# First attention stage: two projection products moved from the head of a turn to places between the score pairs

## The reference, cut to what matters

```python
latent_kv = x @ w_kv_down
k, v = split(latent_kv @ w_kv_up)
q = x @ w_q
att = softmax(where(causal, q @ k.T * 64 ** -0.5, -inf))
y = (att @ v) @ w_out
# beside it, with weights and activations quantised to FP4 in blocks of 16
gate, up = fp4_linear(x, w_gate), fp4_linear(x, w_up)
ffn = fp4_linear(silu(gate) * up, w_down)
x = x + y + ffn
```

## Time and profile before

| | us |
|---|---|
| median of 3 runs | 2572.29 (2571.3 to 2573.58) |
| the profiled execution | 2572.54 |
| its span, first to last instruction | 2570.7 |

### The profile page before, as it was taken

The page is one execution under the profiler, slowest core; times in us unless marked ns, Lnnn a source line. Parts: engine busy times, 40 slices in busy tenths (PEclk is TensorE's granted clock), DMA queues, the critical chain, the costliest instruction groups (busy, mean ns, idle before and its releaser), DMA issues. The chain is left out here.

```text
span 2570.7 us, 49578 instructions
## 1 busy us (share of the span) xinstructions
PE 2252.3 (88%) x19387; PEld 1397.6 (54%) x19387; DVE 1705.0 (66%) x2090; ACT 1371.9 (53%) x2165; POOL 112.4 (4%) x259
## 2 busy tenths in 40 slices
PE   3799999898999999898989955959999999999998
PEld 2466666666666666666666642624444444444444
DVE  8566666666666576666666685067776777777781
ACT  3455555545455554545455541406666566566666
POOL 0100000000000000000000021000000000000000
PEclk8799999999999999999999977959999999999999
DMA  2000000000000000000000007023111111111000
GB/s 75 1 0 0 0 0 0 0 0 0 0 0 0 0 0 0 0 0 0 0 0 0 0 17 175 23 56 59 18 18 25 31 23 18 27 18 32 12 2 10
DMA packets 41101, 41.18 MB, mean 16 GB/s; under 512 B 21393, under 2 KB 33633, under 8 KB 40865
## 3 DMA queue, kind: packets, MB, share of 16 engines
q1 hardware_dynamic: 38904, 36.87, 6.7%
q0 software_dynamic: 640, 1.15, 0.4%
q10 hardware_dynamic: 1448, 1.61, 0.3%
HBM read 26.60 MB, written 11.63 MB: 15 GB/s over the span
## 5 line engine op out<-in xcount | busy, mean ns | idle before, releaser
L1469 DVE TENSOR_REDUCE nm_half<-slot 128x2 f32<-128x1024 f32 x512 | 605.3, 1222 | 184.5 <-PE slot L1318 141.6
L1451 ACT ACTIVATE pT<-slot 128x1024 f32<-128x1024 f32 x512 | 505.7, 1026 | 328.7 <-PE slot L1401 275.0
L473 PE MATMUL slot<-k_hl,q_hl 64*128 64x512 f32 (+3 forms) x2560 | 382.3, 390 | 90.0 <-ACT prob L578 88.8
L578 ACT ACTIVATE prob<-slot,negmax 128x1024 f32<-128x1024 f32 (+6 forms) x448 | 317.7, 725 | 145.4 <-DVE negmax L618 138.5
L473 PEld LDWEIGHTS slot<-k_hl,q_hl 64*128 64x128 f32 x2560 | 291.2, 209 | 136.3 <-issue 84.0
L493 PE MATMUL slot<-ident,prob 128*128 128x128 f32 x2304 | 307.1, 279 | 37.0 <-ACT prob L578 16.8
L587 ACT ACTIVATE probT<-slot 128x1024 f32<-128x1024 f32 x192 | 169.8, 885 | 296.9 <-PE slot L493 296.9
L493 PEld LDWEIGHTS slot<-ident,prob 128*128 128x128 f32 x2304 | 248.9, 141 | 131.9 <-issue 97.8
L618 DVE TENSOR_REDUCE negmax<-slot 128x1 f32<-128x1024 f32 (+2 forms) x192 | 191.8, 1042 | 168.2 <-PE slot L481 167.6
L1313 PE MATMUL slot<-ks,qs 48*128 48x512 f32 x1024 | 255.0, 496 | 49.1 <-DMA ks<-rows 23.2
L505 PE MATMUL yspace<-probT,v_sb 128*64 128x512 f32 (+3 forms) x1536 | 283.0, 496 | 0.0
(11 more groups left out here) (236 smaller groups left out, 2579.6 us busy)
## 6 DMA issues: line engine op xcount, KB each, us to landing
qs<-q_hi SPq DMA_DIRECT2D x64, 64.0 KB
qs<-q_lo SPq DMA_DIRECT2D x64, 64.0 KB
ks<-k_hi SPq DMA_DIRECT2D x60, 64.0 KB
ks<-k_lo SPq DMA_DIRECT2D x60, 64.0 KB
x_tok<-in_L_attn_x_dram SPq DMA_DIRECT2D x4, 512.0 KB, 7.3
q_hi<-qk_out SPq DMA_DIRECT2D x4, 512.0 KB, 3.3
q_lo<-qk_out SPq DMA_DIRECT2D x4, 512.0 KB, 4.1
k_hi<-qk_out SPq DMA_DIRECT2D x4, 512.0 KB, 4.1
```

Of the source, the lines that this page charges most:

```text
L473: last = nc.tensor.matmul(own_ps[a][:, o:o + m], q_hl[hq][own, i * P:(i + 1) * P], k_hl[hk][own, o:o + m], start=(k == 0), stop=(k == 3 an ...
L578: last = nc.scalar.activation(prob[a][:, p_at(i, 0, w)], ps[:, o:o + w], ACT.Exp, bias=negmax[:, i, a:a + 1], accum_out=sums[:, i, a:a + 1])
L1451: nc.scalar.activation(pT[hp][m % PT_DEEP][:, :, :], slot[at["x", n] % RING][:, :].rearrange("p (j t) -> p j t", t=BANK), ACT.Exp)\
L1469: nc.vector.tensor_reduce(nm_half[:, h, :, p * TPB + i], slot[pos % RING][:, :].rearrange("p (a t) -> p a t", t=BANK), AX.X, ALU.max, nega ...
```

## The change

In block B the two products leave the head of the turn. `order` now has "v" in front of score tile 4 and "gu" in front of score tile 6; TensorE makes the values product between the second and third score pair and the gates product between the third and fourth; ScalarE copies the values after exponential 3 and takes its two gates steps after exponential 5. The signal `proj_done` moves from the first matmul of the first score pair to the first matmul of the fourth. Nothing is added or removed: the same instructions with the same shapes.

Because slots go by place in `order`, the slots change as well. Each cell names the slot and, in brackets, its holder before:

| tile | before | after |
|---|---|---|
| score 0 | 1 (TK) | 2 (TO of the turn before) |
| score 1 | 2 (TV) | 0 (TQ) |
| score 2 | 0 (TGU) | 1 (TK) |
| TV | 2 (TO of the turn before) | 2 (score 0) |
| score 4 | 1 (score 0) | 0 (score 1) |
| score 5 | 2 (score 1) | 1 (score 2) |
| TGU | 0 (TQ) | 2 (TV) |
| score 6 | 0 (score 2) | 0 (score 4) |
| score 8 | 1 (score 4) | 1 (score 5) |
| score 9 | 2 (score 5) | 2 (TGU) |

From there on, and for tiles 3 and 7 in `yspace`, nothing differs.

```diff
-                TQ, TK, TV, TGU = range(4)
-                TS = 4
+                TQ, TK = range(2)
+                TS = 2
...
-                order = [("s", n) for n in range(NS1)]
+                V_BEFORE, GU_BEFORE = 4, 6
+                order = []
+                for n in range(NS1):
+                    order += ["v"] * (n == V_BEFORE) + ["gu"] * (n == GU_BEFORE) + [("s", n)]
...
+                TV, TGU = at["v"], at["gu"]
...
-                        ps = claim(TV)
-                        for k in range(TPB):
-                            last = nc.tensor.matmul(ps[:, k * P:(k + 1) * P], lat_s[:, k * P:(k + 1) * P], wv_s[:, :], start=True, stop=True)
-                        last.then_inc(full[TV % RING], 1)
-                        ps = claim(TGU)
-                        nc.tensor.matmul(ps[:, 0:I], xq_s[:, :], wguT[:, 0:I], start=True, stop=True)
-                        nc.tensor.matmul(ps[:, BANK:BANK + I], xq_s[:, :], wguT[:, I:2 * I], start=True, stop=True).then_inc(full[TGU % RING], 1)
...
-                                        if n == 0 and k == 0 and o == 0 and a == 0:
+                                        if n == GU_BEFORE and k == 0 and o == 0 and a == 0:
 
                                             last.then_inc(proj_done, 1)
...
                         for n in range(0, NS1, 2):
+                            if n == V_BEFORE:
+                                ps = claim(TV)
+                                for k in range(TPB):
+                                    last = nc.tensor.matmul(ps[:, k * P:(k + 1) * P], lat_s[:, k * P:(k + 1) * P], wv_s[:, :], start=True, stop=True)
+                                last.then_inc(full[TV % RING], 1)
+                            if n == GU_BEFORE:
+                                ps = claim(TGU)
...
                             scores(n)
...
-                        filled(act, it, TV)
-                        frees(nc.scalar.activation(v_sb[:, :, :], slot[TV % RING][:, :].rearrange("p (k c) -> p k c", c=P), ACT.Copy), TV)
-                        filled(act, it, TGU)
...
                         for n in range(NS1):
+                            if n == V_BEFORE:
+                                filled(act, it, TV)
+                                frees(nc.scalar.activation(v_sb[:, :, :], slot[TV % RING][:, :].rearrange("p (k c) -> p k c", c=P), ACT.Copy), TV)
+                            if n == GU_BEFORE:
+                                filled(act, it, TGU)
+                                gu_ps = slot[TGU % RING][:, :].rearrange("p (k c) -> p k c", c=BANK)
+                                nc.scalar.activation(eg[:, :], gu_ps[:, 0, 0:I], ACT.Exp, scale=-1.0)
+                                frees(nc.scalar.activation(gu[:, :, :], gu_ps[:, :, 0:I], ACT.Copy), TGU)
                             exponentials(n)
```

More of the change, by code:

```diff
@@ L485, in body @@
                         for n in range(0, NS1, 2):
+                            if n == V_BEFORE:
[5 more added lines that the diff above has]
+                                ps = claim(TGU)
+                                nc.tensor.matmul(ps[:, 0:I], xq_s[:, :], wguT[:, 0:I], start=True, stop=True)
+                                nc.tensor.matmul(ps[:, BANK:BANK + I], xq_s[:, :], wguT[:, I:2 * I], start=True, stop=True).then_inc(full[TGU % RING], 1)
                             scores(n)
@@ L563, in body @@
                             nc.scalar.activation(dst[0][:, :], slot[n % RING][:, :], ACT.Copy).then_inc(hi_done, 1)
-                        filled(act, it, TV)
-                        frees(nc.scalar.activation(v_sb[:, :, :], slot[TV % RING][:, :].rearrange("p (k c) -> p k c", c=P), ACT.Copy), TV)
-                        filled(act, it, TGU)
-                        gu_ps = slot[TGU % RING][:, :].rearrange("p (k c) -> p k c", c=BANK)
-                        nc.scalar.activation(eg[:, :], gu_ps[:, 0, 0:I], ACT.Exp, scale=-1.0)
-                        frees(nc.scalar.activation(gu[:, :, :], gu_ps[:, :, 0:I], ACT.Copy), TGU)
                         def exponentials(n):
```

## The result

| | before | after |
|---|---|---|
| median, us | 2573.78 (9 runs) | 2580.45 (9 runs) |
| profiled execution's span, us | 2570.7 | 2575.7 |
| first to last mark of L563 (L568 after), us | 1375.7 | 1381.7 |

The changed kernel is slower: ratio 1.0024, 95% interval 1.0014 to 1.0034, about 6 us. The forecast was 2582.5 and slower, in the range 2574 to 2593. With nine runs instead of three the median of the kernel before is 2573.8 instead of 2572.3.

The account below looks back on a forecast made before the run. The prediction took waits on the chain, not TensorE's work, as what the change could move. A short turn of 43.26 + 1.45 = 44.7, less 44.38, gives 0.32 over 32 turns, +10 us: 2582.5 us, range 2574 to 2593.

Parts of the forecast that it names:

- The head: Start of the turn: with both products gone, maxima 0 starts at 182.48 instead of 183.95, a gain of 1.47 us.
- The third pair: Third score pair: waits for exponential 2 instead of 1, starting at 187.21, 0.48 us earlier than 187.69.
- The fourth pair: Fourth score pair: tile 6 waits for exponential 4's slot, so it starts at 191.13, 1.46 us later.
- a hand-off of 0.15: From a slot's release to the waiting pair's first matmul: 0.15 us booked, as seen at 181.72 and 187.69.
- the row of 191.52: Row where TensorE follows a release by 0.06; basis of the quick hand-offs rival, 2576 us, chance 0.15.
- What hides: Moved copy, gates product, its ScalarE steps and staging copies run in waits of block B; all priced at nothing.
- the lower end of its cover: Values product ahead of the third pair: spare time forecast at 0.15 to 0.3 us, any excess on the chain.
- Passing through: From exponential 6 to the turn's end: its delay of 1.45 us passes in full, making a turn 44.7 us.
- The clock: TensorE's clock: full in all turns after the change, with 0 to 1.15 us a turn kept as the bound.
- the ledger of 1.15 a turn: Cost of the slow clock stretch in the kernel before: turns of 43.26 to 44.41, 1.15 us a turn.
- all are shorter: TensorE's remaining holes, about 1.2, 0.9 and 0.5 us, are shorter than 1.94, so full clock was taken.
- The rule on interleaving: Skill advice cited for the rival that the fourth pair isn't held, starting at 190.65: 2567 us, chance 0.04.

Follow-up runs that it names:

- The experiment with the extra wait: The changed kernel with the first score pair also held until k's low part is done: 2633.14 us, ratio 1.0234 to the kernel before.
- the gates-only kernel: The changed kernel with the values product, its number and its copy back at the head, so only the gates product moves: 2588.89 us, ratio 1.0061 to the kernel before.
- the pad of 0.43: The kernel before with one extra 256-column matmul at the head of every turn, ahead of the q product: 2573.78 us, ratio 0.9994.

## Why the prediction was right

*The head.* The gain of 1.47 came as 1.52 (6.90 to 5.38). The experiment with the extra wait confirms how it is made up: 0.94 of it is the first two passes ahead of k's low part.

*The third pair.* Forecast 0.48 earlier than before, measured 0.53. The step that said that an exponential's time is lost since tile 5 stands behind exponential 2 is right, and the gates-only kernel is the counter-proof: there the head is 1.0 later and the pair behind exponential 1, and it starts at the same 10.1.

*The fourth pair.* Forecast 1.46 later, measured 1.31. This is the mis-sized term of the sum. I booked a hand-off of 0.15 as for an idle pair; it measured 546.02 - 545.96 = 0.06, as in the row of 191.52 that I had set aside. How long the pair had stood idle doesn't tell which of the two it is: the third pair after, idle for only 0.16, took 542.20 - 542.06 = 0.14 from the end of exponential 2's accumulator read. With the 0.05 gained at the head, that is the whole 0.13 a turn between 44.7 and 44.57, some 4 us. That it is the slot that holds the pair is shown by two kernels together: with the gates product doubled it does not move, with the slot's holder changed it comes 2.0 earlier.

*What hides.* Values copy, gates product, ScalarE's gates steps, staging copies: all as forecast. The values product had the lower end of its cover, 0.16. The 1.79 that the forecast took off 3.16 for the gates product is the time from the start of the values product to that of the gates, 178.56 to 180.35; the row for the latter isn't among those shown. ScalarE idles 1.01 ahead of exponential 4 and 0.74 ahead of exponential 6 for the maxima, so its moved steps are not on the chain.

*Passing through.* Yes: exponential 6 is 1.31 late and so is the turn, 44.57 - 43.26.

*The clock.* The outcome was right, full clock in all turns, and the ledger of 1.15 a turn was right in the mean: filling the hole gave 34 of the 36 us. The reason was too simple, and the forecast of full clock was in part luck. I argued from the length of holes, "all are shorter". The gates-only kernel has the same hole as before and 25 turns without a slow stretch, and the kernel with the gates product behind the fourth pair has slow stretches behind a hole of 0.90, while its longest hole is the same 1.30 at the head as in the changed kernel. So holes shorter than 1.94 did not vouch for full clock. Nor are 1.15 us a fixed surcharge on a turn: the pad of 0.43 was absorbed. In the kernel with the later gates product a sum like mine (full clock, 44.38 - 44.12 = 0.26 a turn) would have promised 8 us, and it measured none. What sets how often the clock falls stays open.

*The rule on interleaving* (the Trainium skill, "Perfetto Trace Analysis", "Optimization Strategy") says that performance may be improved by interleaving regimes, where the most-contended engine changes over time. Here it went both ways. The values product alone made the kernel 23 us faster, by the clock and not by a shorter chain; the gates product alone made it 15 us slower. What decides here is which slot the moved work takes, a thing that the busy shares don't show.

*Best version.* The kernel before with one spare matmul in the hole, 2539.38 us, beats both by 34 and 41 us.

## What to carry to other kernels

When work is moved within a ring of buffers, write the list of who stands behind whom before and after: here one product moved behind six score tiles made a pair of scores wait for the exponential just ahead of it, 1.3 us a turn, and the moved work itself cost nothing. Before crediting a move with filling a hole, fill the hole with a spare instruction: it prices the clock by itself, and here it was the better change. And where a loop's turns alternate between two lengths, take the clean turn as the ruler; a change of a few tenths in it may not show in the mean at all.

## What the runs showed of the hardware

TensorE's clock fell to the 1.2 GHz level for a stretch in 30 of 32 turns of the kernel before, with a hole of 1.94 ahead of it; in 17 of 32 with the same hole and a turn longer by 0.43; in 7 of 32 with the same hole and a turn longer by 1.3; in 17 of 32 behind a hole of 2.42 at the head of the turn; and in 8 of 32 behind holes of 0.90 and 0.28, which stand in the other 24 turns too. Leaving out the first turns of the loop, one slow stretch made a turn longer by 0.86 us (gates only) to 1.4 us (first pair held for k's low part).

Unexpected was that the mean length of a turn stayed at 44.34 to 44.38 us in three kernels whose undisturbed turns are 43.26, 43.69 and 44.12.

From the end of an exponential's accumulator read to the first matmul that waited for its slot it took 0.06 us for the fourth pair after, with TensorE idle for 0.55, but 0.14 for the third pair after, idle for 0.16, and 0.15 for the third pair before, idle for 1.94.
